# Two heads per product, and V's bias by matmul, in the attention sums of a fused decoder layer

## The reference

```python
H, DH = 16, 8                                    # 16 heads of 8
def retention(x):                                # "ret"
    Q, K, V = heads(x @ Wq + bq), heads(x @ Wk + bk), heads(x @ Wv + bv)
    scores = Q @ K.T / sqrt(DH)
    retained = (scores * decay_mask) @ V         # no softmax
    return layernorm(retained) * gamma_beta * sigmoid(x @ Wg + bg) @ Wo + bo
def cross(x, ctx):                               # "cross": softmax, keys and values of ctx
def self_moe(x):                                 # "self": causal softmax, no biases,
    ...                                          # then 8 experts of width 512, top 2
x = layernorm(x + retention(x)); x = layernorm(x + cross(x, ctx)); x = layernorm(x + self_moe(x))
```

## Time and profile before

| what | value |
|---|---|
| median of 3 runs | 1304.31 us (1303.89 to 1305.38) |
| the profiled execution | 1301.8 us |
| its span, first to last instruction | 1300.5 us |
| mean granted TensorE clock | 0.890 |
| PE busy, products | 1073.4 us, 17677 |
| PE weight loads (PEld) busy | 762.5 us |
| DVE, ACT, POOL busy | 857.1, 822.0, 912.2 us |

### The profile page before, as it was taken

The page is one execution under the profiler, slowest core; times in us unless marked ns, Lnnn a source line. Parts: engine busy times, 40 slices in busy tenths (PEclk is TensorE's granted clock), DMA queues, the critical chain, the costliest instruction groups (busy, mean ns, idle before and its releaser), DMA issues.

```text
span 1300.5 us, 45997 instructions
## 1 busy us (share of the span) xinstructions
PE 1073.4 (83%) x17677; PEld 762.5 (59%) x17677; DVE 857.1 (66%) x2370; ACT 822.0 (63%) x1884; POOL 912.2 (70%) x859
## 2 busy tenths in 40 slices
PE   5888888788999888889888988847787799999562
PEld 2555555554555555555555555537777789999310
DVE  4677776766788786777666677445444466666485
ACT  2345554678999886777777776315534466666377
POOL 3788888866766657777777766765656756677596
PEclk9999898988999997999888898568889999999876
DMA  5465332222232223222222221111212233332453
GB/s 159 125 184 149 85 86 63 65 58 55 75 92 77 82 63 84 66 67 68 77 68 64 77 72 41 52 34 43 61 55 64 66 85 99 95 101 78 143 163 97
DMA packets 132181, 108.61 MB, mean 84 GB/s; under 512 B 19563, under 2 KB 122476, under 8 KB 131932
## 3 DMA queue, kind: packets, MB, share of 16 engines
q1 hardware_dynamic: 123548, 88.29, 24.8%
q0 software_dynamic: 8416, 17.38, 3.8%
HBM read 41.58 MB, written 26.75 MB: 53 GB/s over the span
## 4 chain that ended last, share of the span: by engine, by line
PE 45%; ACT 15%; issue 15%; POOL 9%; DVE 8%; DMA 4%; SPq 1%; another core or an unknown queue 1%; DVEq 1%; ACTq 0%; POOLq 0%
PE bank L1201 8%; PE bank L1210 7%; ACT Kz L687 4%; PE bank L547 4%; PE bank L612 3%; POOL Plo L769 3%; PE bank L550 3%; PE bank L450 2%; PE bank L510 2%; PE bank L487 2%; PE bank L517 2%; DMA xrow<-block_rows 2%; PE bank L443 2%; DVE P L841 2%; ACT P L726 2%
## 5 line engine op out<-in xcount | busy, mean ns | idle before, releaser
L769 POOL TENSOR_TENSOR Plo<-P 128x1024 f16<-128x1024 f32 x192 | 363.9, 1897 | 166.6 <-ACT P L726 138.3
L1253 POOL DMA_INDIRECT expert_rows<-yo,ix x135 | 174.8, 1295 | 100.1 <-DVE ix L1247 67.9
L1224 ACT ACTIVATE G<-bank,we 128x128 f32<-128x128 f32 x540 | 154.7, 370 | 98.9 <-PE bank L1201 83.0
L817 DVE TENSOR_REDUCE mx<-bank 128x16 f16<-128x1024 f32 x128 | 156.7, 1224 | 35.0 <-PE bank L465 32.8
L687 ACT ACTIVATE Kz<-kh,col 128x512 f16<-128x512 f16 x256 | 167.1, 718 | 0.1
L1210 PE MATMUL bank<-we,G 128*128 128x128 f32 x1080 | 149.6, 283 | 17.5 <-issue 11.8
L510 PE MATMUL bank<-Vh,P 64*128 64x17 f16 (+1 forms) x3072 | 152.3, 170 | 14.0 <-issue 13.7
L726 ACT ACTIVATE P<-bank 128x1024 f32<-128x1024 f32 x128 | 131.1, 1024 | 48.2 <-PE bank L487 27.8
L787 POOL DMA_INDIRECT block_rows<-xs,slots x128 | 133.4, 1042 | 40.1 <-issue 38.2
L512 PE MATMUL bank<-Vl,P 64*128 64x16 f16 x3072 | 149.3, 167 | 11.5 <-issue 11.5
L1201 PE MATMUL bank<-hTb,we 128*128 128x128 f32 x1080 | 151.1, 285 | 8.0 <-issue 4.1
(11 more groups left out here) (187 smaller groups left out, 2165.4 us busy)
## 6 DMA issues: line engine op xcount, KB each, us to landing
Qz<-qh SPq DMA_DIRECT2D x192, 64.0 KB, 2.0
Kst<-kh SPq DMA_DIRECT2D x192, 64.0 KB
xrow<-block_rows SPq DMA_DIRECT2D x135, 65.0 KB
y_t<-expert_rows SPq DMA_DIRECT2D x16, 512.0 KB, 4.1
Qz<-ql SPq DMA_DIRECT2D x96, 64.0 KB, 2.0
Kst<-kl SPq DMA_DIRECT2D x96, 64.0 KB
xT<-xt SPq DMA_DIRECT2D x16, 256.0 KB, 2.7
xs<-x SPq DMA_DIRECT2D x16, 256.0 KB, 4.0
```

The costliest lines, as they stand in the source:

```text
L769: pool.tensor_tensor(Plo[n % 3][:, :], P32[n % 3][:, :], upper(n), ALU.subtract).then_inc(f_Pl.of(n), 1)
L817: dve.tensor_reduce(columns, bank[:, S_BANK:S_BANK + 2, :].rearrange("p r (j i k) -> p r j i k", i=2, k=S), AX_X, ALU.max, negate=True).th ...
L1224: i = act.activation(G[b][:, c, :], bank[:, 2 + p, c * P:(c + 1) * P], ACT.Gelu_apprx_tanh, bias=we[b][:, B1 + c:B1 + c + 1])
L1253: pool.indirect_dma_start(ydst[:, :], bass.IndirectOffsetOnAxis(ix2[s % 4][:, :], 0), yo[s % 4][:, :], None).then_inc(b_sc.of(s), 16)
```

## The change

- `Vh` and `Vl` get one more axis of two and become block-diagonal: in partitions of sequence `b` only part `b` is filled, the other stays zero, and the ones column stands only in its own part. All buffers are cleared once at the start; then POOL writes the ones columns.
- `pe_sums` contracts over all 128 partitions: one product per head pair and term, 24 per tile in place of 48, with 34 (or 32) columns in two parts `b`. A tile's results stand in one bank (`PV_BANK + t % 2`), with strides of 34 and 17.
- `act_values` and `dve_values` fill the two diagonal blocks with an instruction each of 64 partitions, in all three kinds, from `bankB`.
- In the retention `V32`, its DVE addition and `f_V32` go. The bias is split once, by ten small dependent POOL operations, into three bf16 rows; before V's projection PE multiplies a matrix of ones with 3 rows by them into `bankB` over 512 columns, and the four projections accumulate on it. PE's waits on `f_V32` become waits on `f_Vl`.

```diff
-    V32 = sb("V32", [P, GW])
-    Vh = [sb(f"Vh{p}", [P, GT, 8, 2 * DH + 1], F16) for p in range(3)]
-    Vl = [sb(f"Vl{p}", [P, GT, 8, 2 * DH], F16) for p in range(3)]
+    bias_left = [sb(f"bias_left{p}", [3, P]) for p in range(2)]
+    bias_part = [sb(f"bias_part{p}", [3, P], BF16) for p in range(3)]
...
+    Vh = [sb(f"Vh{p}", [P, GT, 8, 2, 2 * DH + 1], F16) for p in range(3)]
+    Vl = [sb(f"Vl{p}", [P, GT, 8, 2, 2 * DH], F16) for p in range(3)]
...
-    for b in [*Qz, *Kst, *mx, *Vh]:
+    for b in [*Qz, *Kst, *mx, *Vh, *Vl]:
...
+    pool.wait_ge(s_set, settings)
+    for v in Vh:
+        for b in range(2):
+            pool.memset(v[64 * b:64 * b + 64, :, :, b, 2 * DH], 1.0).then_inc(s_set, 1)
+            settings += 1
...
+    pool.wait_ge(l_ident, 16)
+    value_bias = row[0:3, ROWS.index("a_bv"), :]
+    pool.tensor_copy(bias_part[0][:, :], value_bias).then_inc(s_bias, 1)
+    pool.wait_ge(s_bias, 1)
+    pool.tensor_tensor(bias_left[0][:, :], value_bias, bias_part[0][:, :], ALU.subtract).then_inc(s_bias, 1)
...
+    for p in range(3):
+        pool.tensor_scalar(bias_own[p][:, :], bias_part[p][:, :], ident[0:3, p:p + 1], None, ALU.mult).then_inc(s_bias, 1)
...
+    pool.tensor_tensor(bias_rows[:, :], bias_sum[:, :], bias_own[2][:, :], ALU.add).then_inc(s_bias, 1)
+    BIAS_DONE = 10
...
     def pe_sums(n):
+        taken = bank[:, PV_BANK + t % 2, 0:8 * 2 * (2 * DH + 1)].rearrange("p (c b e) -> p c b e", b=2, e=2 * DH + 1)
...
         for c in range(8):
             cs = slice(c * P, (c + 1) * P)
-            for b in range(2):
-                rows_b = slice(64 * b, 64 * b + 64)
-                at = (t % 2) * 256 + c * 32
-                o = bank[:, PV_BANK + b, at:at + nv]
-                pe.matmul(o, up[rows_b, cs], Vh[g % 3][rows_b, t, c, 0:nv], start=True, stop=False)
-                pe.matmul(o, lo[rows_b, cs], Vh[g % 3][rows_b, t, c, 0:nv], start=False, stop=False)
-                i = pe.matmul(o[:, 0:2 * DH], up[rows_b, cs], Vl[g % 3][rows_b, t, c, :], start=False, stop=True)
+            o = taken[:, c, :, :]
+            pe.matmul(o[:, :, 0:nv], up[:, cs], Vh[g % 3][:, t, c, :, 0:nv], start=True, stop=False)
+            pe.matmul(o[:, :, 0:nv], lo[:, cs], Vh[g % 3][:, t, c, :, 0:nv], start=False, stop=False)
+            i = pe.matmul(o[:, :, 0:2 * DH], up[:, cs], Vl[g % 3][:, t, c, :, :], start=False, stop=True)
...
-                pe.wait_ge(*(f_V32 if kind(g - 1) == "ret" else f_Vl)(g - 1))
+                pe.wait_ge(*f_Vl(g - 1))
...
+            if not plain:
+                pe.matmul(bankB, onesb[0:3, :], bias_rows[:, :].unsqueeze(1).broadcast_to([3, GT, P]), start=True, stop=False)
             for t in range(GT):
                 i = pe.matmul(bankB[:, t * P:(t + 1) * P], source_of(g)[:, t * P:(t + 1) * P], weights_of(g)["V"],
-                              start=True, stop=True)
+                              start=plain, stop=plain or t == GT - 1)
...
+        act.wait_ge(*f_V(g))
+        for b in range(2):
+            rows_b = slice(64 * b, 64 * b + 64)
+            i = act.copy(Vh[g % 3][rows_b, :, :, b, 0:2 * DH].rearrange("p t c e -> p (t c) e"),
+                         bankB[rows_b, :].rearrange("p (c e) -> p c e", e=2 * DH))
...
-            dve.tensor_tensor(V32[:, :].rearrange("p (t d) -> p t d", d=P), bankB.rearrange("p (t d) -> p t d", d=P), brow("a_bv"),
-                              ALU.add).then_inc(f_V32.of(g), 1)
...
+        for b in range(2):
+            rows_b = slice(64 * b, 64 * b + 64)
+            i = dve.tensor_tensor(Vl[g % 3][rows_b, :, :, b, :].rearrange("p t c e -> p (t c) e"),
+                                  bankB[rows_b, :].rearrange("p (c e) -> p c e", e=2 * DH),
+                                  Vh[g % 3][rows_b, :, :, b, 0:2 * DH].rearrange("p t c e -> p (t c) e"), ALU.subtract)
```

More of the change, by code:

```diff
@@ L223, in build @@
         "xTs", "gate", "qh", "kh", "Vh", "mTs", "OTs", "On", "y", "Kz"))
-    f_ql, f_kl, f_V32, f_Vl, f_r = (count(f"f_{n}") for n in ("ql", "kl", "V32", "Vl", "r"))
+    f_ql, f_kl, f_Vl, f_r = (count(f"f_{n}") for n in ("ql", "kl", "Vl", "r"))
+    s_bias = ctx.enter_context(nc.semaphore("s_bias"))
     f_st, f_mv = ([count(f"f_{n}{j}") for j in range(2)] for n in ("st", "mv"))
@@ L500, in pe_sums @@
         if kind(g) == "ret":
-            pe_keep_clock(bank[:, PV_BANK, (t % 2) * 256:(t % 2) * 256 + 256], 1)
+            pe_keep_clock(bank[:, PV_BANK + t % 2, 0:256], 1)
         pe.wait_ge(*f_Pl(n))
@@ L693, in act_values @@
         act.wait_ge(*f_PV(GT * (g - 3) + GT - 1))
-        if kind(g) == "ret":
-            act.wait_ge(*f_V32(g))
-            v = V32[:, :]
-        else:
-            act.wait_ge(*f_V(g))
-            v = bankB
-        act.copy(Vh[g % 3][:, :, :, 0:2 * DH].rearrange("p t c e -> p (t c) e"),
-                 v.rearrange("p (c e) -> p c e", e=2 * DH)).then_inc(f_Vh.of(g), 1)
+        act.wait_ge(*f_V(g))
[3 more added lines that the diff above has]
+                         bankB[rows_b, :].rearrange("p (c e) -> p c e", e=2 * DH))
+        i.then_inc(f_Vh.of(g), 1)
     def act_maxima(g):
@@ L847, in results @@
         g, pair = n // GT, n // 2
-        pv = bank[:, PV_BANK:PV_BANK + 2, :].rearrange("p b (t c e) -> p b t c e", t=2, e=32)
+        pv = bank[:, PV_BANK:PV_BANK + 2, 0:8 * 2 * (2 * DH + 1)].rearrange("p t (c b e) -> p b t c e", b=2, e=2 * DH + 1)
         rd = rden[pair % 2]
```

28 lines of the change are left out of this document (19 added, 9 removed).

## The result

The kernel became slower: 1324.5 us (median of 4 runs, 1321.2 to 1328.6) against 1304.1 us (4 runs, 1303.2 to 1305.4), ratio 1.0177, 95% interval 1.0139 to 1.0215. I had said 1279, and the range ended at 1308. The profiled execution took 1321.2 us (span 1319.9, mean granted clock 0.897).

A forecast was written before the change was run, and what follows sets the result against it. Engines waiting on each other bound retention, ACT the seven cross groups, PE with issue stalls the later groups. -8.6 + 3.4 - 20 - 6 + 5 + 0.5 = -25.7 us gave 1279 us, range 1246 to 1308.

The forecast's parts named there:

- The sums on PE: Per tile, 24 products of 128 rows at 26 ns: 0.79 us against 0.79 us now, nothing gained or lost.
- Rival C: Sums' outputs in two runs cost PE, doubling the 26 ns step: slower, +6.9 us in total, 1311 us; chance 0.15.
- Borders: PE's switches between 64-row and 128-row array use around the sums: 0.09 us saved at each border removed.
- the mixed groups: The 25 cross and self groups with routing: stalls -20, borders -6, second halves +5 us; -21 in the forecast table.
- The bias path: Retention without V32: ACT's Vh no longer waits for DVE; the loop gains 0.3 us, -8.6 us in all with borders.
- The second halves: Extra Vh and Vl instructions in cross and self groups, mostly hidden in idle time: +5 us for 25 groups, bounds 0 and +28.
- cross alone: Seven cross groups bound by ACT: a second Vh copy adds 0.49 us each, +3.4 us, bounds 0 and +5.
- The stalls, -20: PE's instruction-issue gaps at the sums in 25 cross and self groups: halved instruction demand saves 20 us, bounds 0 and -45.
- Rival B: Instruction supply truly bounds the last stretch; all 45 us of stall go, on the path: 1251 us, chance 0.20.
- D: Rival: the stalls at PE's sums have a fixed length, so the -20 falls away: 1299 us, chance 0.15.
- The start, +0.5: POOL's larger memsets and bias rows delay PE's first V product, partly regained: +0.5 us, bounds 0 and +2.

The follow-up runs named there:

- e10: The kernel before with V's bias by three bf16 rows and ACT's Vh copy one key block earlier, nothing block-diagonal: 1257.7 us, ratio 0.9887.
- e4: The kernel before with only V's bias by a product of three bf16 rows; single Vh and Vl instructions, 64-row sums: 1290.1 us, ratio 0.9896.
- e1: The kernel before with Vh and Vl each made in two 64-partition instructions in cross and self groups, nothing else: 1340.5 us, ratio 1.0306.
- e2: The changed kernel without the second halves of Vh and Vl in cross and self groups, so part of the computation is missing: 1283.3 us, ratio 0.9853.
- e11: The kernel before with Vh alone made in two halves in cross and self groups, Vl one instruction: 1328.6 us, ratio 1.0243.
- e12: The kernel before with Vl alone made in two halves in cross and self groups, Vh one instruction: 1326.9 us, ratio 1.0242.
- e15: The changed kernel with a semaphore for each half of Vh, so DVE's first half need not wait for both: 1314.2 us, ratio 1.0154.
- r3: The changed kernel run once more, unaltered, in another set, against the kernel before: 1327.2 us, ratio 1.0264.

## Why the prediction was wrong

**The sums on PE: right.** 26 ns per step and 0.77 us per tile, nothing gained in the stream of products. Rival C (two-run outputs slow PE) is refuted. The Trainium skill, PSUM — Partial Sum Buffer, section Specifications, says that any non-contiguous access slows matmuls significantly; outputs in two runs of 16 at a stride of 17 kept the 26 ns of contiguous ones, so the measurement decides.

**Borders: right in size for one** (0.10 us for 0.09). In the retention the new sums took 6 us less for the forecast 4, but e10 gets as short without them; in the mixed groups, where I had put -6, no gain shows.

**The bias path: right, and too small.** Waits and order came as described; -9.9 us alone (e4), -12.6 in the whole change, for -8.6 with the borders in it. The bias product takes 0.31 us (138.81 to 139.12), not 0.22. The bounds, 0 and -25, held it.

**The second halves: the step that failed most.** I had written "both have idle time, so a third: +5", with +28 as the bound, and for cross alone +3.4 from ACT only. Measured: +35.2 when added (e1), -33.7 when taken out (e2). The idle time of ACT and DVE lies elsewhere. At this place ACT's second copy, DVE's first half (held by one semaphore for both), DVE's second half and DVE's `mx` follow each other, and PE needs `Vl` for its keep-clock product in `bankB` and `mx` for its next work. About half of the price is PE idle, and half is the same products at a lower granted clock. My own bound, +28 for 25 groups and +5 for 7, nearly held the measured price; the choice of a third did not, because I never asked what stands behind `Vl` on DVE. The length of a half, 0.49 and 0.6 us of new work, was about right: what failed was to call it hidden.

**The stalls, -20: failed.** The gaps shrank as forecast (10.8 us for 12), but they did not set the length: the softmax stretch of the kernel before is 571.7 us with 34.7 us of them and with 1.4. Presumably they stood in front of other waits. The last groups gave 7 us, mostly a halt of DVE that I had not priced. Rival B, all 45 on the path, was the farthest off; D's outcome in the mixed groups, no gain, came true for another reason. What spoke for D, ACT's halts before `P`, was real: 20.2 us went to 5.0, and DVE has such halts too.

**The start, +0.5: failed by 6.5.** The six memsets of ones columns took 1.65 us where I had about 0.9, and POOL's operations 0.28 to 0.60 us where I took 0.20 to 0.35, so V's projection started 3.6 us late. The other 3.4 us are PE's products at half their pace and the bias product, which the sum did not have.

In the sum: -8.6 came out as -12.6, +3.4 as +8.4, -21 as +24.6 - 7.1 = +17.5, +0.5 as +7.0; with the two small rows of the table the miss is 45.1 us, of which the mixed groups make 38.5. No rival described the mechanism; my slower one stood on another.

**Open.** Why e11 and e12 are not additive. Why the changed kernel's softmax stretch is 604.7 and 605.5 us where there are gaps before the sums and 594.0 where there are none, when that of before is 571.7 on both kinds of chip; only that the granted clock differs with it (0.85, 0.85 and 0.88) is seen. What halts DVE at the end. And whether the waits lower the clock. I had taken it as unchanged, and it was 0.91 and 0.85 in the later two windows (0.95 and 0.91 before), but 1.00 in the retention (0.92 before). In e15, where PE waits less, the mean is 0.908 against 0.890 of r3 in the same set, so the lower clock may follow from the waits and add to them; no run separates the two.

## What to carry to other kernels

An instruction split by partitions was here not two halves but two whole ones: count each at full length, in series, and follow the engine's own order behind it (here `Vl`, then `mx`, then PE) before calling it hidden in idle time. Idle time before an instruction is a gain to be had only if nothing else would have held it; the test is the length of the stretch in a run that lacks the gaps. A named wait shows where to look, not the price: leave the suspected work out, as e2 does, and compare the stretch, after asking how far it spreads in kernels that share its code. And take a change that couples several edits apart: the bias path with ACT's copy one block earlier (e10, 0.9887) is faster than both kernels in its set.
